# Eight instead of five split down blocks per tile of a routed feed-forward layer, with two norm chains joined

## The reference, cut to what matters

```python
x = x + layernorm(attention(layernorm(x)))       # 16 heads of 8
x = x + layernorm(ffn(layernorm(x)))

def ffn(x):
    # 32 experts of 64, 6 of them per token out of 4 of 8 groups, weights root-summed to 2.5
    h = relu(einsum('th,eih->tei', x, up_w)) ** 2 * combine[:, :, None]
    return einsum('tei,ehi->th', h, down_w) + (relu(x @ shared_up.T) ** 2) @ shared_down.T
```

## Time and profile before

| | us |
|---|---|
| median of three runs | 509.29 |
| the three runs | 506.84, 510.2, 509.29 |
| the profiled execution's own time | 507.4 |
| its span, first to last instruction | 505.6 |
| PE busy in the span | 461.5 (91%) |
| DVE busy | 392.6 (78%) |
| ACT busy | 360.2 (71%) |
| POOL busy | 232.2 (46%) |

### The profile page before, as it was taken

One profiled execution on the slowest core, in us unless ns is written; L12 is line 12 of the kernel. 1 busy time (PEld: TensorE's weight loads), 2 busy tenths in 40 slices (PEclk: granted clock), 3 DMA queues, 4 the chain that ended last, 5 costly groups with the idle time before them and its releaser, 6 DMA issues.

```text
span 505.6 us, 10660 instructions
## 1 busy us (share of the span) xinstructions
PE 461.5 (91%) x3328; PEld 265.6 (53%) x3328; DVE 392.6 (78%) x1013; ACT 360.2 (71%) x723; POOL 232.2 (46%) x551
## 2 busy tenths in 40 slices
PE   2467999999999999998899899999999999999994
PEld 2222444444444444543346566666666666666662
DVE  3688888889899889989726969595977869596453
ACT  3314888888989888887847586878788777867552
POOL 7055333336555635320113646748384664716351
PEclk9999999999999999999979999999999999999998
DMA  7543344444444444420024263456253544535331
GB/s 205 161 135 120 116 122 124 145 141 145 136 123 149 141 144 138 135 68 3 3 102 160 82 206 132 168 147 211 101 186 117 152 167 177 183 107 209 128 103 41
DMA packets 49047, 67.45 MB, mean 133 GB/s; under 512 B 3808, under 2 KB 35808, under 8 KB 48992
## 3 DMA queue, kind: packets, MB, share of 16 engines
q1 hardware_dynamic: 48992, 66.78, 41.2%
HBM read 51.17 MB, written 15.20 MB: 131 GB/s over the span
## 4 chain that ended last, share of the span: by engine, by line
PE 75%; DVE 10%; issue 8%; ACT 5%; POOL 1%; DMA 0%; POOLq 0%; DVEq 0%; ACTq 0%
PE pO L1282 10%; PE pS L1224 9%; PE pY L1363 8%; PE pS L1363 8%; PE pS L1347 6%; PE pS L1348 6%; PE pS L1349 6%; DVE mneg L926 6%; PE pS L1230 3%; PE pX L1209 2%; PE pY L1299 2%; ACT probs L709 2%; PE pX L1212 2%; PE pY L1311 2%; DVE q_rest L906 1%
## 5 line engine op out<-in xcount | busy, mean ns | idle before, releaser
L926 DVE TENSOR_REDUCE mneg<-pS 128x2 f32<-128x512 f32 x256 | 162.7, 685 | 16.5 <-PE pS L1224 15.8
L709 ACT ACTIVATE probs<-pS 128x512 f32<-128x512 f32 x256 | 142.5, 596 | 25.8 <-PE pS L1230 24.1
L1224 PE MATMUL pS<-qk 48*128 48x256 bf16 x512 | 87.9, 288 | 17.7 <-DVE mneg L926 9.2
L794 ACT ACTIVATE h_ring<-r 128x512 f32<-128x512 f32 x104 | 64.3, 624 | 36.9 <-DVE r L1071 26.4
L1230 PE MATMUL pS<-qk 51*128 51x256 bf16 x512 | 88.6, 280 | 2.2 <-ACT probs L709 2.2
L1347 PE MATMUL pS<-qk,up_hi 128*128 128x512 f32 x144 | 88.5, 614 | 0.0
L1282 PE MATMUL pO<-probs,vv 128*32 128x256 f32 x1024 | 73.6, 394 | 0.0
L1224 PEld LDWEIGHTS pS<-qk 48*128 48x128 bf16 x512 | 33.5, 96 | 69.4 <-DVE mneg L926 46.6
L1071 DVE SCALAR_TENSOR_TENSOR r<-pS,probs 128x512 f32<-128x512 f32 x64 | 43.6, 689 | 27.4 <-PE pS L1349 26.5
L1349 PE MATMUL pS<-qk,up_lo 128*128 128x512 f32 x144 | 56.9, 395 | 0.0
L1348 PE MATMUL pS<-qk,up_hi 128*128 128x512 f32 x144 | 56.9, 395 | 0.0
(11 more groups left out here) (188 smaller groups left out, 812.4 us busy)
## 6 DMA issues: line engine op xcount, KB each, us to landing
c_ring<-c_scratch SPq DMA_DIRECT2D x32, 512.0 KB, 3.9
probs<-c_scratch SPq DMA_DIRECT2D x32, 512.0 KB, 3.8
qk<-qk_scratch SPq DMA_DIRECT2D x64, 192.0 KB
qk_scratch<-q_parts SPq DMA_DIRECT2D x16, 192.0 KB, 2.3
qk_scratch<-k_parts SPq DMA_DIRECT2D x16, 192.0 KB, 2.3
qk_scratch<-q_parts SPq DMA_DIRECT2D x16, 128.0 KB, 2.2
qk_scratch<-k_parts SPq DMA_DIRECT2D x16, 128.0 KB, 2.1
out_x<-probs SPq DMA_DIRECT2D x7, 256.0 KB, 4.6
```

Of the source, the lines that this page charges most:

```text
L709: nc.scalar.activation(probs[j][:, hh], pS2[n % S2_RING][:, :, :], ACT.Exp, scale=SCALE).then_inc(exp_done, 1)
L794: nc.scalar.activation(h_ring[:, (n - at) % HRING], r_sb[n % URING][:, :], ACT.Square).then_inc(sq_done, 1)
L926: nc.vector.tensor_reduce(mneg[u % 2][:, :, hh, k], pS1[n % S1_RING][:, :].rearrange("p (a s) -> p a s", a=TH), AX.X, ALU.max, negate=True ...
L1224: return mm(pS1[n % S1_RING][:, T * th:T * (th + 1)], qp[slot][rows, k, P * th:P * (th + 1)], kp[slot][rows, k, :], start=True, stop=True)
```

## The change

- `SPLIT` becomes (2, 3, 5, 6, 8, 11, 12, 14): per tile ten plain and eight split down blocks, in place of thirteen and five. The rings of `h_hi` and the whole grow from 3 to 4, that of `h_lo` from 2 to 3, with the new buffers laid into attention's `probs` and `qk`.
- The weights of the three new split blocks are split by a second `split_down`, 128 x 512, behind GpSimd's first root_of_sum; the parts lie in attention's `qk` buffers.
- The chains of y (tile i + 3) and f (tile i - 1) are joined in tiles 1 to 4: ten operations on 128 x 8 in place of twenty on 128 x 4; the last one, the shift, stays in two pieces with a semaphore each.
- VectorE's statistics of y move from k = 15 to k = 9.
- GpSimd's queue in tile i (from 1 on) becomes: low 0, low 1, residual1, root_of_sum, low 2, low 3, chain x1, low 4, joined chain (in tiles 5 to 7 chain f alone), low 5, low 6, low 7, residual2. In tile 0: low 0, low 1, residual1, low 2, low 3, root_of_sum, chain x1, low 4, chain y, low 5, low 6, low 7.

```diff
-SPLIT = (2, 5, 8, 11, 14)
-SPLIT_LAG, HI_RING, LO_RING = 6, 3, 2
+SPLIT = (2, 3, 5, 6, 8, 11, 12, 14)
+SPLIT_LAG, HI_RING, LO_RING = 6, 4, 3
...
-        work2, work3, work4 = ([sb(f"work{k}_{n}", [P, C4]) for n in "vtmdh"] for k in (2, 3, 4))
+        work3, work24 = ([sb(f"work{k}_{n}", [P, c]) for n in "vtmdh"] for k, c in ((3, C4), (24, 2 * C4)))
+        work2, work4 = ([w[:, C4 * i:C4 * (i + 1)] for w in work24] for i in range(2))
...
+        spare2 = probs[5][:, :, :, :].rearrange("p a b c -> p (a b c)")
+        h_whole = [h_ring[:, HRING], spare[:, 0:TILE], spare[:, TILE:2 * TILE], spare2[:, 0:TILE]]
...
             if not fused:
                 link(eng.tensor_tensor(rs, v, power[:, 0:v.shape[-1]], ALU.pow))
+                for cols, done in parts:
+                    eng.tensor_tensor(nm[:, cols], m[:, cols], rs[:, cols], ALU.mult).then_inc(done, 1)
+                if parts:
+                    return
                 return eng.tensor_tensor(nm, m, rs, ALU.mult)
...
+            def chain_y_and_f(i, n):
+
+                pool.wait_ge(y_stats, i + 1)
+                pool.wait_ge(f_stats, n + 1)
+                pool.wait_ge(yn_done, i)
+                if n >= 1:
+                    pool.wait_ge(fn_done, n)
+                link = Link(pool, ln2_link, LN_LINKS * i)
+                norm_chain(nc.gpsimd, pool.wait_ge, link, stats24[:, :, :], [w[:, :] for w in work24],
+                           rs24[:, :], nm24[:, :], parts=((slice(0, C4), ln2_done), (slice(C4, 2 * C4), ln4_done)))
...
-            def split_down():
+            def split_down(part):
                 pool.wait_ge(down_loaded, 16 * NCUT)
-                nc.gpsimd.tensor_copy(down_hi[:, :, :], down_whole).then_inc(dhi_done, 1)
-                pool.wait_ge(dhi_done, 1)
-                nc.gpsimd.tensor_tensor(down_lo[:, :, :], down_whole, down_hi[:, :, :].bitcast(F32),
+                if part == 1:
+                    pool.wait_ge(s2_done, 2 * UB * (NU - 2))
+                nc.gpsimd.tensor_copy(down_hi[part], down_whole[part]).then_inc(dhi_done, 1)
+                pool.wait_ge(dhi_done, part + 1)
+                nc.gpsimd.tensor_tensor(down_lo[part], down_whole[part], down_hi[part].bitcast(F32),
                                         ALU.subtract).then_inc(dlo_done, 1)
...
             root_of_sum(0)
+            split_down(1)
             chain_y(2)
             for i in range(NTILE):
                 low(i, 0)
+                low(i, 1)
                 if i + 2 < NTILE:
                     residual1(i + 2)
+                if i >= 1 and i + 1 < NTILE:
+                    root_of_sum(i + 1)
+                low(i, 2)
+                low(i, 3)
                 if i == 0:
-                    low(i, 1)
-                    low(i, 2)
-                if i + 1 < NTILE:
                     root_of_sum(i + 1)
-                if i >= 1:
-                    low(i, 1)
                 if i + 2 < NTILE:
                     chain_x1(i + 2)
-                if i >= 1:
-                    low(i, 2)
-                if i >= 1:
+                low(i, 4)
+                if i >= 1 and i + 3 < NTILE:
+                    chain_y_and_f(i + 3, i - 1)
+                elif i >= 1:
                     chain_f(i - 1)
-                low(i, 3)
-                low(i, 4)
-                if i + 3 < NTILE:
+                else:
                     chain_y(i + 3)
+                low(i, 5)
+                low(i, 6)
+                low(i, 7)
                 if i >= 1:
                     residual2(i - 1)
...
-                    if i + 3 < NTILE and k == 15:
+                    if i + 3 < NTILE and k == 9:
                         stats_y(i + 3)
...
-                mm(pF[i % 2], down_hi[:, s], high, start=False, stop=False)
-                mm(pF[i % 2], down_lo[:, s], high, start=False, stop=False)
-                mm(pF[i % 2], down_hi[:, s], low, start=False, stop=s == len(SPLIT) - 1).then_inc(split_done, 1)
+                third, part = divmod(k - SBLK, 3)
+                w_hi, w_lo = down_hi[part][:, third], down_lo[part][:, third]
+                mm(pF[i % 2], w_hi, high, start=False, stop=False)
+                mm(pF[i % 2], w_lo, high, start=False, stop=False)
+                mm(pF[i % 2], w_hi, low, start=False, stop=s == len(SPLIT) - 1).then_inc(split_done, 1)
```

More of the change, by code:

```diff
@@ L143, in block_kernel @@
         idb = sb("idb", [P, P], BF16)
-        stats, stats2, stats3, stats4 = (sb(n, [P, c, 6]) for n, c in (
-            ("stats", NT), ("stats2", C4), ("stats3", C4), ("stats4", C4)))
+        stats, stats24, stats3 = (sb(n, [P, c, 6]) for n, c in (("stats", NT), ("stats24", 2 * C4), ("stats3", C4)))
+        stats2, stats4 = stats24[:, 0:C4], stats24[:, C4:2 * C4]
         rs1, nm1 = sb("rs1", [P, NT]), sb("nm1", [P, NT])
-        rs2, nm2 = sb("rs2", [P, C4]), sb("nm2", [P, C4])
+        rs24, nm24 = sb("rs24", [P, 2 * C4]), sb("nm24", [P, 2 * C4])
+        rs2, nm2, rs4, nm4 = rs24[:, 0:C4], nm24[:, 0:C4], rs24[:, C4:2 * C4], nm24[:, C4:2 * C4]
         rs3, nm3 = sb("rs3", [P, C4]), sb("nm3", [P, C4])
-        rs4, nm4 = sb("rs4", [P, C4]), sb("nm4", [P, C4])
         nw_v, nw_t, nw_m, nw_d, nw_h = (sb(f"nw_{n}", [P, NT]) for n in "vtmdh")
-        work2, work3, work4 = ([sb(f"work{k}_{n}", [P, C4]) for n in "vtmdh"] for k in (2, 3, 4))
+        work3, work24 = ([sb(f"work{k}_{n}", [P, c]) for n in "vtmdh"] for k, c in ((3, C4), (24, 2 * C4)))
+        work2, work4 = ([w[:, C4 * i:C4 * (i + 1)] for w in work24] for i in range(2))
         tiny = sb("tiny", [P, 2])
@@ L202, in block_kernel @@
         spare = probs[4][:, :, :, :].rearrange("p a b c -> p (a b c)")
-        h_whole = [h_ring[:, HRING], spare[:, 0:TILE], spare[:, TILE:2 * TILE]]
+        spare2 = probs[5][:, :, :, :].rearrange("p a b c -> p (a b c)")
+        h_whole = [h_ring[:, HRING], spare[:, 0:TILE], spare[:, TILE:2 * TILE], spare2[:, 0:TILE]]
         h_hi, h_lo = ([sb(f"{name}{i}", [P, TILE], F32R)[:, :] for i in range(n)]
-                      for name, n in (("h_hi", HI_RING), ("h_lo", LO_RING)))
-        down_hi, down_lo = (sb(f"down_{n}", [P, len(SPLIT), D], F32R) for n in ("hi", "lo"))
-        down_whole = down_sb[:, :, :].rearrange("p (a b) d -> p a b d", b=3)[:, 0:len(SPLIT), 0]
+                      for name, n in (("h_hi", HI_RING - 1), ("h_lo", LO_RING - 1)))
+        for ring, slot in ((h_hi, 4), (h_lo, 5)):
+            ring.append(qk[slot][:, UB // 2:UB].rearrange("p j a b -> p (j a b)").bitcast(F32R))
+        down_hi, down_lo = ([sb(f"down_{n}", [P, 5, D], F32R)[:, :, :],
+                             qk[slot][:, 0:UB // 2].rearrange("p j a b -> p (j a b)").bitcast(F32R)
+                             .rearrange("p (s d) -> p s d", d=D)] for n, slot in (("hi", 4), ("lo", 5)))
+        down_thirds = down_sb[:, :, :].rearrange("p (a b) d -> p a b d", b=3)
+        down_whole = [down_thirds[:, 0:5, 0], down_thirds[:, 0:4, 1]]
         fT_sb = sb("fT_sb", [P, TILE])
-        assert all(k - SBLK == 3 * s for s, k in enumerate(SPLIT))
         assert (HRING + 1) * TILE == RBLK * P and TILE >= SI
@@ L336, in part3, with norm_chain @@
                               ALU.subtract).then_inc(part3_done, 1)
-        def norm_chain(eng, wait, link, st, work, rs, nm, before_write=None, fused=False):
+        def norm_chain(eng, wait, link, st, work, rs, nm, before_write=None, fused=False, parts=()):
             v, t, m, d, half = work
@@ L519, in split_max, with norm @@
                                         ALU.subtract).then_inc(mparts_done, 1)
-            def norm(i, link_sem, stats_sem, st, work, rs, nm, used, ready):
-                link = Link(pool, link_sem, LN_LINKS * i)
+            def norm(i, link_sem, stats_sem, st, work, rs, nm, used, ready, links_from=0):
+                link = Link(pool, link_sem, LN_LINKS * (i - links_from))
                 pool.wait_ge(stats_sem, i + 1)
-                norm_chain(nc.gpsimd, pool.wait_ge, link, st[:, :, :],
-                           [w[:, :] for w in work], rs[:, :], nm[:, :],
+                norm_chain(nc.gpsimd, pool.wait_ge, link, st,
+                           work, rs, nm,
                            (used, i) if i >= 1 else None).then_inc(ready, 1)
@@ L547, in chain_x1 @@
             def chain_x1(i):
-                norm(i, ln3_link, x1_stats, stats3, work3, rs3, nm3, xn2_done, ln3_done)
+                norm(i, ln3_link, x1_stats, stats3[:, :, :], [w[:, :] for w in work3], rs3[:, :], nm3[:, :],
+                     xn2_done, ln3_done)
             def chain_f(i):
-                norm(i, ln4_link, f_stats, stats4, work4, rs4, nm4, fn_done, ln4_done)
+                norm(i, ln4_link, f_stats, stats4, work4, rs4, nm4, fn_done, ln4_done, NTILE - 4)
+            def chain_y_and_f(i, n):
[7 more added lines that the diff above has]
+                           rs24[:, :], nm24[:, :], parts=((slice(0, C4), ln2_done), (slice(C4, 2 * C4), ln4_done)))
+                assert link.n == LN_LINKS
```

(7 more changed lines are left out.)

## The result

The changed kernel takes 524.49 us (median of four runs, 523.57 to 525.08), the kernel before 509.75 beside it: 1.031 times as long, 95% interval 1.027 to 1.035. The forecast was 520.5, range 512 to 527. The profiled execution took 523.57 with a span of 521.8, 16.2 more than the 505.6 of before.

What follows compares the result with a forecast made beforehand. TensorE bounds at 29.06 us per tile, a loop through VectorE and GpSimd 0.69 behind; the change makes that loop 31.41. Terms 0.3 + 2.6 + 9.4 + 1.5 - 0.2 - 0.5 = +13.1 on 507.4 give 520.5 us, range 512 to 527.

Steps and rivals of the forecast that it cites:

- TensorE bounds the tile by 0.69 only: Kernel before: TensorE's 29.06 us per tile against a 28.37 us loop through VectorE, GpSimd and TensorE.
- GpSimd, order: GpSimd's queue from routing sum to low 5's first matmul: 13.57 us, with one more low part and a widened chain.
- TensorE's piece: TensorE from low 5's first matmul to the next tile's block 1: 4.04 plus 0.68 for split block 12, 4.72 us.
- VectorE's piece: VectorE from block 1 to routing sum: 12.92 us plus 0 to 0.69 of holds by GpSimd, taken as 0.2.
- Tiles 1 to 4: Loop of 31.41 us per tile against 29.06 before: +2.35 each, +9.4 for the four.
- Tile 5: Loop with chain f alone, 0.85 less: 30.56 us, +1.5.
- Tile 0: Block 1 of tile 1 comes at 299.0 less 0.2, instead of 296.20: +2.6 us (2.2 to 3.0).
- Tile 6: No chain x1: TensorE's own 27.2 us with some 0.3 of waiting for low 2, -0.2.
- End of attention: Second split of weights behind the first root: its cast can hold an operation, 0 to 0.6 us, taken as 0.3.
- TensorE stays the bound: Rival: TensorE still bounds the tiles, time falls by 8 x 0.51 = 4.1 us to 503.3; chance 0.07.
- In part: Rival: VectorE's work from block 1 to sum shrinks 1 to 2 us; +3 to +8, 510 to 515; chance 0.09.
- VectorE is held more: Rival: low 1 holds the selection's operations longer, another 0.5 to 1 us per tile, 525 to 530; chance 0.07.

Runs made afterwards that it cites:

- run 4: Kernel before plus two idle 128 x 512 subtractions on GpSimd between the root and low 1, tiles 1 to 5; 523.65 us, 1.031.
- run 1: Changed kernel with the chains apart in tiles 1 to 4: chain f in the joined chain's place, chain y behind low 7; 520.64 us, 1.023.
- run 2: Changed kernel with low 2 ahead of residual1 and low 3 ahead of the root from tile 1 on, joined chain kept; 529.99 us, 1.042.
- run 5: Kernel before plus two idle 128 x 512 subtractions on GpSimd behind low 0, beside VectorE's routing; 514.31 us, 1.012.
- run 7: Kernel before with seven split blocks (2, 5, 8, 11, 13, 14, 15), chains apart, new low parts behind low 3; 517.37 us, 1.018.
- run 3: Changed kernel with run 2's reordering and the chains apart, chain y behind low 7 in tile 0 too; 527.39 us, 1.037.
- run 8: Kernel before with eight split blocks (2, 5, 8, 11, 13, 14, 15, 16), chains apart, otherwise as run 7; 518.78 us, 1.021.
- run 9: Changed kernel with the chains apart, low 4 ahead of chain x1 and low 5 ahead of chain f; 527.78 us, 1.038.
- run 10: Changed kernel with low 4 ahead of chain x1 and low 5 ahead of the joined chain; 528.05 us, 1.039.
- run 11: Changed kernel with chain x1 between low 2 and low 3 in tiles 1 to 7; 533.32 us, 1.051.

## Why the prediction was right

- **TensorE bounds the tile by 0.69 only.** Right that the margin is small, wrong in the place: over low 1 it was 0.19 (run 4). It didn't touch the sum, since that was worked out for low 5, where the loop did close.
- **GpSimd, order.** Predicted 13.57 from sum to low 5's matmul, measured 13.43; the joined chain 4.02, measured 388.86 - 384.81 = 4.05, with a power of 1.67 as reckoned from the widths in the earlier trace rows. That the join adds 0.85 here was shown by run 1 (0.90).
- **TensorE's piece.** Predicted 4.72, measured 4.84. Its waits came at steps 10, 11, 14 and 17, most at 17 (0.81).
- **VectorE's piece** was the mis-sized term: 12.92 + 0.2, measured 13.33. Of the two reasons given for the 0.2, the one of L1020 beside residual1 didn't come: L1020 took 0.74 before, and L1048, the same operation now, takes 0.76. The other, low 1 beside the selection of groups, did, and at 0.4: the copy L1008 takes 0.74 instead of the 0.17 of L980, the same operation before, and ends at 370.62, with low 1, which runs from 369.30 to 370.59. Low 1 after, and the copy before:

```profile
369.30 1.29 POOL L623 TENSOR_TENSOR h_lo<-probs,h_hi 128x512 fp32r<-128x512 f32 x1 [0.73 <-ACT h_hi L813]
```

```profile
360.96 0.17 DVE L980 COPY g_best<-top 128x16 f32<-128x16 f32 x1
```

  The Trainium skill's page "SBUF — State Buffer", section "Who interferes with whom", says that VectorE's copies in a two-port mode contend with GpSimd's operations, as its operations with two inputs in SBUF do, and that whichever was issued first blocks the other. The prediction gave 0.4 per tile for it, by an estimate from that page, and left it out because no row showed it. The rows agree with the page: the copy lost 0.57, L1032 (L1004 before) was held for 0.15 less than in the earlier trace rows, and 0.4 remains. The long holds of runs 2, 5 and 7 agree with it too.
- **Tiles 1 to 4:** 31.41 predicted, 31.60 to 31.66 measured, +10.2 instead of +9.4. *Tile 5:* 31.05 against 30.56, from the same pieces (13.34, 12.87, 4.84); the middle one has 0.3 more because one operation of chain x1 there takes 0.51 instead of 0.20. *Tile 0:* +3.1 against +2.6; its sum came 0.5 later instead of 0.2 earlier. *Tile 6:* +0.45 against -0.2; block 1 to sum 12.87, to low 2's matmul (472.99) 2.42, to block 1 of tile 7 12.88, together 28.17, the tile. The wait of 0.3 for low 2 came as foretold, but I added it to TensorE's own length instead of adding up the path behind it. *End of attention:* 0.3 taken; it can't be told from the scatter.
- **The rivals.** "TensorE stays the bound" fell: the waits on low parts are there. "In part" fell: VectorE's piece grew. "VectorE is held more" has its mechanism in the trace, at 0.2 instead of 0.5 to 1 per tile on top of the forecast's 0.2. Of the 4 us between 520.5 and the measured median 2.5 are these pieces of tiles 0 to 7; the rest lies ahead of the feed-forward stage and in the scatter of the runs.

What the prediction didn't see is how many loops are nearly as long as TensorE's own tile. With these eight blocks, low 5 allows 31.6, chain x1 through ScalarE 30.5; GpSimd's work at other places falls beside the routing (runs 2, 3, 5, 7, 8), and another order behind the sum lengthens another path (9, 10, 11). No version run here is faster than the kernel before, and no run removes the hold itself, so what eight blocks would give without it stays open.

## What to carry to other kernels

Before work is moved to an engine with free time, list every path that leaves its queue and returns to the engine that bounds, and read each path's slack at its own consumer: here TensorE's own work and two such paths lay within 0.7 us, and the smallest slack (0.19) was not on the path that I had read. Free time on GpSimd beside VectorE operations on SBUF isn't free: a 1.3 us operation cost VectorE up to 1.1, so it belongs where VectorE idles or reads TensorE's banks (its rectifiers stay at 0.69 in every row here). A joined chain delays whatever stands behind it: it cost 0.90 per tile ahead of low 5 (run 1), and behind low 5 it cost nothing and gained nothing (run 10 beside run 9).

## What the runs showed of the hardware

The granted clock can fall right behind a stretch in which TensorE stood still for some 2 us in one piece, but doesn't each time. Windows of run 11: TensorE's wait, then the work behind it, in tile 3, then the same two stretches in tile 4.

```profile
383.00:387.00 4.00, 2.17 (x9) 1.07 (x7) 4.00 (x10) 2.92 (x8) 3.59 (x9) 1.00 0.47 132
388.00:391.40 3.40, 3.40 (x8) 2.00 (x7) 0.69 (x1) 1.51 (x4) 3.02 (x10) 0.52 0.38 148
...
417.00:421.00 4.00, 2.17 (x9) 1.16 (x8) 4.00 (x9) 2.91 (x7) 3.62 (x8) 1.00 0.41 131
421.70:425.10 3.40, 3.40 (x15) 2.43 (x14) 1.38 (x2) 2.00 (x5) 3.02 (x10) 1.00 0.57 166
```

At 0.52 (near the 1.2 GHz level) a plain block lasts 1.91 instead of 1.02:

```profile
388.66 1.91 PE L1393 MATMUL pY<-h_ring,down_sb 128*128 128x512 f32 x2
```

The tile loses 1.6 us by it (33.69 against 32.09). Outside run 8, tiles with a mean clock below 1.00 appear only in the runs where TensorE has one wait of 1.8 to 2.6 us per tile (2, 3, 4 and 11) or two of 1.0 and 0.8 close together (9 and 10); in run 4, whose waits of 2.2 us come in every tile, two of five:

```profile
297.44:328.92 31.48, 29.28 (x113) 19.57 (x112) 22.88 (x74) 22.68 (x44) 19.70 (x40) 1.00 0.51 166
328.92:362.04 33.12, 30.96 (x113) 20.44 (x112) 22.85 (x74) 22.84 (x44) 21.43 (x41) 0.95 0.43 137
```

In run 8 it is tiles 0 and 1 (0.96 and 0.93): the clock falls behind a wait of 1.77 us near the end of tile 0. Run 7 has a wait of 1.78 us at the same place and keeps 1.00. The changed kernel, which spreads 1.8 us of waits over four places in tile 3, keeps 1.00 in tiles 0 to 6. Which of two equal waits is followed by the drop, the runs don't tell.
